# Last layer as one block: the last head group takes half of the sequences first, and the experts start on that half

## The reference, cut to what matters

```
h = rmsnorm(x, ln1_w);  q, k, v = h @ wq, h @ wk, h @ wv          # 16 heads of 128
attn = softmax(where(causal, q @ k.T / sqrt(128), -1e9))
x = x + (attn @ v) @ wo                                            # within each of the 4 sequences
h = rmsnorm(x, ln2_w);  probs = softmax(h @ gate_w.T)              # 16 experts
cw = top 6 of probs, divided by their sum
hh = silu(h @ eg_w.T) * (h @ eu_w.T);  routed = sum_e cw[e] * hh @ ed_w.T
out = x + routed + silu(h @ sg_w.T) * (h @ su_w.T) @ sd_w.T
```

## Time and profile before

| What | us |
|---|---|
| median of three runs | 934.74 |
| the profiled execution | 932.43 |
| its span | 930.7 |
| PE busy | 776.9 (83%) |
| DVE busy | 572.8 (62%) |
| ACT busy | 413.7 (44%) |
| POOL busy | 238.0 (26%) |

### The profile page before, as it was taken

How to read it: one execution, slowest core, us unless ns; L and a number is a source line. 1 busy time by engine, 2 the same in 40 slices (tenths; PEclk the granted TensorE clock), 3 DMA queues, 4 the chain that set the end, 5 groups by cost and what they waited for, 6 DMA issues and landing times. The chain is left out here.

```text
span 930.7 us, 11234 instructions
## 1 busy us (share of the span) xinstructions
PE 776.9 (83%) x3633; PEld 581.3 (62%) x3633; DVE 572.8 (62%) x1269; ACT 413.7 (44%) x856; POOL 238.0 (26%) x245
## 2 busy tenths in 40 slices
PE   1986685887864465999999999999989999999995
PEld 0433454444542155878888787887777888888883
DVE  6997999979989874556555565555635323233333
ACT  6894111244414655545464354543533334343331
POOL 5310101500042412102111021120021555555452
PEclk9998997889977776999999999999977999999998
DMA  4000005723120003011010110000022241333411
GB/s 144 3 0 1 0 0 197 288 69 137 46 73 0 1 1 130 6 46 46 1 46 1 46 46 1 1 1 1 1 69 66 74 114 57 92 78 80 95 38 45
DMA packets 37374, 49.85 MB, mean 54 GB/s; under 512 B 18670, under 2 KB 30038, under 8 KB 35654
## 3 DMA queue, kind: packets, MB, share of 16 engines
q1 hardware_dynamic: 36262, 46.90, 16.5%
q0 software_dynamic: 768, 2.10, 0.7%
q10 hardware_dynamic: 288, 0.14, 0.1%
HBM read 43.00 MB, written 6.13 MB: 53 GB/s over the span
## 5 line engine op out<-in xcount | busy, mean ns | idle before, releaser
L2273 DVE TENSOR_TENSOR B_l<-bank,TW_l 128x512 f32<-128x512 f32 (+1 forms) x50 | 34.6, 692 | 141.0 <-PE bank L2218 141.0
L1891 ACT ACTIVATE EX<-EX,nm 128x128 f32<-128x128 f32 (+1 forms) x128 | 57.2, 448 | 108.5 <-DVE nm L1940 108.0
L1841 POOL TENSOR_TENSOR WL<-RAW,WH 128x512 fp32r<-128x512 f32 x32 | 41.1, 1289 | 228.9 <-ACT WH L1865 228.9
L2308 POOL TENSOR_TENSOR HL_l<-H_l,HH_l 128x512 fp32r<-128x512 f32 (+1 forms) x50 | 64.1, 1283 | 115.2 <-ACT HH_l L2287 115.2
L2218 PE MATMUL bank<-XH,WH_l 128*128 128x512 f32 (+1 forms) x200 | 80.0, 400 | 0.0
L2218 PE MATMUL bank<-XH,WL_l 128*128 128x512 f32 (+1 forms) x200 | 79.7, 399 | 0.0
L2218 PE MATMUL bank<-XL,WH_l 128*128 128x512 f32 (+1 forms) x200 | 79.7, 399 | 0.0
L2295 ACT ACTIVATE S_l<-bank 128x512 f32<-128x512 f32 (+1 forms) x50 | 30.1, 601 | 84.2 <-PE bank L2218 84.2
L1954 DVE TENSOR_TENSOR AL<-bank,AH 128x256 fp32r<-128x256 f32 x64 | 27.1, 424 | 62.1 <-ACT AH L1906 62.1
L155 POOL TENSOR_TENSOR WV<-EUK,V 128x512 f32<-128x512 f32 x16 | 23.7, 1488 | 148.8 <-DVE GAIN L244 114.1
L1995 PE MATMUL bank<-XH,WH 128*128 128x512 f32 x128 | 59.7, 466 | 1.3 <-DVE XL L1695 1.3
(11 more groups left out here) (306 smaller groups left out, 2076.4 us busy)
## 6 DMA issues: line engine op xcount, KB each, us to landing
RAW<-l_attn SPq DMA_DIRECT2D x8, 1024.0 KB, 4.9
WE<-l_experts SPq DMA_DIRECT2D x1, 6144.0 KB, 23.0
RAW_l<-l_experts SPq DMA_DIRECT2D x9, 512.0 KB, 3.8
TW_l<-routed SPq DMA_DIRECT2D x16, 256.0 KB, 5.1
RAW<-l_w SPq DMA_DIRECT2D x3, 1024.0 KB
TW_l<-routed SPq DMA_DIRECT2D x14, 192.0 KB, 3.2
RAW_l<-l_experts SPq DMA_DIRECT2D x9, 256.0 KB, 4.6
sorted_x<-ZERO SPq DMA_DIRECT2D x1, 1920.0 KB, 8.1
```

The costliest lines, as they stand in the source:

```text
L1841: pool.tensor_tensor(WL[:, slot, c], RAW[:, slot, c], WH[:, slot, c].bitcast(F32), ALU.subtract).then_inc(w_low, 1)
L1891: act.activation(EX[:, s, a:b], EX[:, s, a:b], ACT.Exp, bias=nm[:, s, i:i + 1], scale=scale, accum_out=rs[:, s, i:i + 1]).then_inc(expd, 1)
L2273: v.tensor_tensor(self.B[0:rows, q % 2], self.k.banks[2 * (q % 2) + 1][0:rows], self.TW[0:rows, w % self.TWS, n * W:(n + 1) * W], ALU.mult ...
L2308: pool.tensor_tensor(self.HL[0:rows, q % 4], self.H[0:rows, q % 2], self.HH[0:rows, q % 4].bitcast(F32), ALU.subtract).then_inc(self.h_low, 1)
```

## The change

The three blocks become one, `layer3`, so that no engine waits for all others between attention, experts and store. Tiles XH, XL, HN, RAW, WH and WL serve both parts; HH and HL lie where Q and K lay.

The last group has its own list. Its units 0 to 3 are both heads of sequences 0 and 1, units 4 to 7 those of sequences 2 and 3; W0 and W1 are the full output of the first half of tokens. Q (squares), M (sums and means), R (roots and reciprocals) and X (spread, normalise, split) are the second normalisation of that half. ACT splits the first expert's weights in the same group.

```
+LAST_PLAN = """S0 C4 S1 N0 C5 C6 N1 T0 C7 T1 S2 A0 C8 S3 N2 A1 C9 N3 T2 C10 T3 A2 C11 A3
+    S4 W0 S5 W1 N4 Q0 S6 N5 T4 M0 S7 N6 T5 A4 N7 T6 A5 R0 T7 A6 X0 A7 W2 W3""".split()
+LAST_MADE = [0, 1, 2, 3, 4, 5, 8, 10, 6, 7, 9, 11]
+def unit(g, n):
+    return ((n // 2) % 2, 2 * (n // 4) + n % 2) if is_last(g) else (n // 4, n % 4)
+def out_chunk(g, n):
+    return (n % 2, n // 2) if is_last(g) else (n // 2, n % 2)
```

```
+STEPS3[1], STEPS3[2] = STEPS3[2], STEPS3[1]
+ROUTE3, OWN3 = 2, (10, 12, 14, 16)
 # PE, after the last group
+            pe.wait_ge(added, 4 * GROUPS)
+            pe.wait_ge(normb.xl, 2)
+            def ahead(q):
+                if q == ROUTE3:
+                    pe.wait_ge(normb.xl, 4)
+                if q == ROUTE3 + 2:
+                    pe.wait_ge(rt, 10 + 2 * NT)
...
+                    for t in range(NT):
+                        mm = pe.transpose(banks[t // 4][0:EXPERTS3, (t % 4) * P:(t % 4 + 1) * P], CW[:, t], k.IDF[:])
...
+                    pe.wait_ge(rows, 2)
+            def behind(q):
+                if q == 0:
+                    normb.add_up(pe, 1)
+                if q == 1:
+                    normb.spread_out(pe, 1)
...                                                     # router logits into banks[6]
+                if q == 2:
+                    pe.wait_ge(normb.xn, 4)
+                    pe.wait_ge(rt, 2)
 # ACT, after the last group
+            act.wait_ge(added, 4 * GROUPS)
+            normb.squares(act, 1)
+            normb.roots(act, 1)
+            normb.high(act, 1)
+            act.wait_ge(scores, 8 * GROUPS)
+            def ahead(q):
+                if q == ROUTE3:
+                    act.wait_ge(rt, 2)
+                    act.activation(PR[:], LG[:], ACT.Exp).then_inc(ex_, 1)
+                if q == ROUTE3 + 2:
+                    for n in range(2):
+                        act.wait_ge(cw_turned, n + 1)
+                        act.activation(ROWW[:, n * W:(n + 1) * W], banks[n][0:EXPERTS3], ACT.Copy).then_inc(rows, 1)
 # DVE
+            for q in range(len(STEPS3)):
+                if q == ROUTE3:
+                    ex.product(v, q - 1)
+                    routed()
+                ex.weigh(v, q)
+                if q >= 1 and q != ROUTE3:
+                    ex.product(v, q - 1)
+                if q in OWN3:
+                    own(OWN3.index(q))                   # X = X + XC, one chunk
+            ex.product(v, len(STEPS3) - 1)
+            v.wait_ge(owned, NCH)
+            for n, j in enumerate(ORDER):
+                v.wait_ge(ex.down, len(STEPS3) - 1 + n // 2)
+                v.tensor_tensor(chunk(k.X[:], j), chunk(k.X[:], j), banks[4 + j][:], ALU.add).then_inc(summed, 1)
```

More of the change, by code:

```diff
@@ L1646, in __init__ @@
+class Norm:
+    def __init__(self, name, sem, k, tiles, col, sum_banks, spread_banks):
+        self.k, self.t, self.col, self.sum_banks, self.spread_banks = k, tiles, col, sum_banks, spread_banks
         self.sq, self.sums, self.mean, self.root, self.rec, self.spread, self.xn, self.xh, self.xl = [
             sem(f"{n}_{name}") for n in "sq sums mean root rec spread xn xh xl".split()]
-    def squares(self, act, k):
-        for j in ORDER:
-            act.activation(chunk(self.SQ[:], j), chunk(k.XC[:], j), ACT.Square).then_inc(self.sq, 1)
@@ L1655, in scalar @@
[L1655 to L1661, removed]
-            act.wait_ge(self.xn, i + 1)
[L1664 to L1674, removed]
-            j = ORDER[i]
[L1677 to L1690, removed]
@@ L1692, in low, with squares @@
-    def low(self, v, n):
[L1693 to L1714, removed]
+    def squares(self, act, n):
+        for j in ORDER[2 * n:2 * n + 2]:
+            act.activation(chunk(self.t.SQ[:], j), chunk(self.k.XC[:], j), ACT.Square).then_inc(self.sq, 1)
@@ new lines, in add_up, with means @@
+    def add_up(self, pe, n):
+        pe.wait_ge(self.sq, 2 * n + 2)
+        for t in range(4):
+            at = (4 * n + t) * P
+            for h in range(KD):
+                mm = pe.matmul(self.sum_banks[n][:, t:t + 1], self.t.SQ[:, h, at:at + P], self.k.ONES[:, 0:1],
+                               start=(h == 0), stop=(h == KD - 1))
+        mm.then_inc(self.sums, 1)
+    def means(self, v, n):
+        t = slice(4 * n, 4 * n + 4)
+        v.wait_ge(self.sums, n + 1)
+        v.tensor_scalar(self.t.ms[:, t], self.sum_banks[n][:, 0:4], 1.0 / D, EPS3, ALU.mult, ALU.add).then_inc(self.mean, 1)
@@ new lines, in roots, with factors, spread_out @@
+    def roots(self, act, n):
+        t = slice(4 * n, 4 * n + 4)
+        act.wait_ge(self.mean, n + 1)
+        act.activation(self.t.rt[:, t], self.t.ms[:, t], ACT.Sqrt).then_inc(self.root, 1)
+    def factors(self, v, n):
+        t = slice(4 * n, 4 * n + 4)
+        v.wait_ge(self.root, n + 1)
+        v.reciprocal(self.t.rstd[:, t], self.t.rt[:, t]).then_inc(self.rec, 1)
+    def spread_out(self, pe, n):
+        pe.wait_ge(self.rec, n + 1)
+        for t in range(4):
+            mm = pe.matmul(self.spread_banks[n][:, t * P:(t + 1) * P],
+                           self.t.rstd[:, 4 * n + t:4 * n + t + 1].to_broadcast([P, P]), self.k.IDF[:], start=True,
+                           stop=True)
+        mm.then_inc(self.spread, 1)
@@ new lines, in normalise, with high @@
+    def normalise(self, v, n):
+        v.wait_ge(self.spread, n + 1)
+        for j in ORDER[2 * n:2 * n + 2]:
+            v.scalar_tensor_tensor(chunk(self.t.HN[:], j), chunk(self.k.XC[:], j),
+                                   self.t.LN[:, self.col, j // 2:j // 2 + 1], self.spread_banks[n][:], ALU.mult,
+                                   ALU.mult).then_inc(self.xn, 1)
+    def high(self, act, n):
+        for i in (2 * n, 2 * n + 1):
+            act.wait_ge(self.xn, i + 1)
+            j = ORDER[i]
+            act.activation(chunk(self.t.XH[:], j), chunk(self.t.HN[:], j), ACT.Copy).then_inc(self.xh, 1)
@@ L1717, in each_group @@
+    def low(self, v, n):
+        for i in (2 * n, 2 * n + 1):
+            v.wait_ge(self.xh, i + 1)
+            j = ORDER[i]
+            v.tensor_tensor(chunk(self.t.XL[:], j), chunk(self.t.HN[:], j), chunk(self.t.XH[:], j).bitcast(F32),
+                            ALU.subtract).then_inc(self.xl, 1)
 def each_group(eng, body):
@@ L2290, in scalar @@
             p = q - FIRST3[i]
+            ahead(q)
             act.wait_ge(self.gate_up, q + 1)
@@ L2344, in layer3_experts @@
         routed_d = nc.dram_tensor("routed4", (EXPERTS3 + 1, T), F32).ap()
[L2345 to L2351 removed]
+        norm = Norm("l3a", sem, k, tiles, 0, (banks[0], banks[3]), (banks[1], banks[2]))
@@ new lines, in layer3 @@
+        normb = Norm("l3b", sem, k, tiles, 1, (banks[0], banks[4]), (banks[1], banks[5]))
+        raw_in = [sem("raw_in0_3"), sem("raw_in1_3")]
+        (ln_in, mask, w_high, w_low, proj, evac0, evac1, scores, rowmax, negmax, expd, recd, normed, turned,
+         pt, av, ah, al, wo, added) = [sem(n + "_3") for n in """ln_in mask w_high w_low proj evac0 evac1 scores
+            rowmax negmax expd recd normed turned pt av ah al wo added""".split()]
+        r_in, logits, rt, ex_, cw_turned, rows, sent, owned, summed, stored = [
+            sem(n + "_4") for n in ("r_in", "logits", "route", "exps", "turned", "rows", "sent", "owned", "summed", "stored")]
@@ L2353, in layer3_experts, with evacuate @@
+        def evacuate(eng, g, n, do):
+            c = made(g, n)
+            eng.wait_ge(proj, 12 * g + n + 1)
+            if later(g):
+                if c < 4:
+                    eng.wait_ge(scores, 8 * (g - 1) + 4)
+                elif c < 8:
+                    eng.wait_ge(av, 8 * g)
+                else:
+                    eng.wait_ge(scores, 8 * g)
+            do(target(c), banks[n % 2][:]).then_inc(evac[n % 2], 1)
         block = ctx.enter_context(nc.Block())
@@ L2374, in _, with split_high @@
             ex.gpsimd(pool)
+        def split_high(act, g, count, slot, m):
+            act.wait_ge(raw_in[slot], 16 * count)
+            if not isinstance(g, int) or g >= 2:
+                act.wait_ge(wo, 4 * (g - 1))
+            c = slice(m * GCOL, (m + 1) * GCOL)
+            act.activation(WH[:, slot, c], RAW[:, slot, c], ACT.Copy).then_inc(w_high, 1)
         @block.scalar
         def _(act):
-            norm.squares(act, k)
-            for part in range(3):
-                ex.split_high(act, 0, part)
@@ L2381, in _ @@
-            norm.scalar(act, k)
-            act.wait_ge(rt, 2)
-            act.activation(PR[:], LG[:], ACT.Exp).then_inc(ex_, 1)
-            for n in range(2):
-                act.wait_ge(turned, n + 1)
-                act.activation(ROWW[:, n * W:(n + 1) * W], banks[5 + n][0:EXPERTS3], ACT.Copy).then_inc(rows, 1)
-            ex.scalar(act)
+            for n in range(2):
+                norm.squares(act, n)
+            for m in range(4):
+                split_high(act, 0, 1, 0, m)
+            for n in range(2):
+                norm.roots(act, n)
@@ new lines, in _, with evacuated, body @@
```

(69 more changed lines are left out.)

679 lines of the change are left out of this document (309 added, 370 removed).

## The result

The changed kernel takes 929.84 us (median, 928.65 to 930.30), the kernel before beside it 934.90: a ratio of 0.9942, 95% interval 0.9929 to 0.9956, so 5.1 us or 0.6% faster. The profiled execution took 930.3, its span 928.6; it counts among the four. Medians here are over all executions, and the ratios leave out those in a slower state of the chip (two of "store only", one of the kernel before).

The account below looks back on a forecast made before the run. PE sets the end wherever its queue is full, so gains lie in transition and tail: -5.3 (transition) - 4.35 (store) + 2.5 (clock) = -7.15, giving 927.6 us against the 934.74 median; range 921.5 to 932.5, own range 925 to 930.

Parts of the forecast that it names:

- rival B: Transition gives nothing, waits in the last group and DRAM trip undersized by 2 to 3 us each; 930 to 932; chance 0.16.
- step 0 at 41: Sign of being right: first expert step starts some 41 us after the last group's first score matmul, before 55.6.
- step 6 at 77.5: Sign of being right: first plain steady expert step starts 77.5 us after the last group's first score matmul, before 82.8.
- a last group longer than 42 us: Sign of being wrong: the last group of heads, forecast to end at t = 40.3, takes over 42 us.
- The store: End of kernel: two adds beside down 49, two follow; 3.8 us after the last matmul in place of 8.2, 4.35 won.
- The transition: Last group to steady expert steps, without a block end and half the tokens first: step 6 at 77.5 against 82.8, 5.3 won.
- ahead of W2: PE, done at t = 34.75, waits 2.7 us for the last head's subtraction, behind normalisation work on DVE's queue.
- ahead of step 4: PE waits 2.15 us, from t = 63.8, for ACT's copies to ROWW.
- ahead of down 3: PE waits 3.15 us: weights return from DRAM at t = 72.7, then weigh 4, product 3, copy and POOL's 1.28.
- The clock: Half clock on PE after three waits over 2 us in dense work; taken as 2.5 us lost, bounds 0 and 15.
- Rival A: The clock never falls or the waits are shorter: -9.65 and a bit, 922 to 925 us; chance 0.17.
- C: Rival: PE stays at half clock for 10 us after each of three waits, 15 lost, +5.4, 940 us; chance 0.07.

Follow-up runs that it names:

- store only: Kernel before with only the store's part: XC added into X beside expert steps 10 to 16, four closing adds instead of eight; 932.58 us, ratio 0.9968.
- old tail: Changed kernel with the end of before: no adds of XC into X beside the steps, eight adds in a row after the last down product; 934.36 us, ratio 1.0001.
- product 3 first: Changed kernel with one swap on DVE, product 3 ahead of weigh 4; 923.96 us, ratio 0.9885.
- filled wait: Changed kernel with 10 matmuls of 512 columns, into a bank nothing reads any more, in PE's wait ahead of W2; 930.39 us, ratio 0.9959.

## Why the prediction was right in size and wrong in its parts

Forecast 927.6, measured 929.84: inside 921.5 to 932.5, and faster, to which I gave 0.82. But it lies just under rival B's 930 to 932, whose account ("only the store is won") is what the traces show. That the time still fell inside the range is luck: the store alone gives 930.4, which lies in it too. Of the signs I named, step 0 at 41 and step 6 at 77.5 did not come (44.7 and 82.7), and one of the signs of being wrong did: a last group longer than 42 us.

- **The store**: 4.35 forecast, 4.2 in the trace (8.2 to 4.0). Right, and the runs bear it out: with the old tail the gain is nil; the adds alone, on the kernel before, give 2.5.
- **The transition**: 5.3 forecast before the clock, measured 0.1 with it. This is the step that failed. Its waits were the right ones, in the right places and with the right causes (ahead of W2 2.7 said, 2.64 measured; ahead of step 4 2.15 and 1.68; ahead of down 3 3.15 and 3.76; trip from the copies to the landing 6.8 and 7.1). What was mis-sized is the list between them, and step 6 came 5.2 later than I said:
  - Up to step 0, 3.5. W2 came at t = 39.7, not 37.5: the second half of the group started at 20.3, not 18.9, and lost another 0.9 up to W2. The half clock over W2 and W3 added 1.3. I take it that the hand-overs from PE to DVE or ACT and back, which I had rounded to the modelled ends of the instructions, add up over the dozens in the group; that was not tested by itself.
  - From step 0 to the landing of the weights, 0.8 (32.3 for 31.5). DVE took 5.2 us from Exp to the weights, where I had taken 4.24 from before. Two of its instructions are the difference: the making of CW took 0.87 and its scaling 0.71, both 0.29 before. In the changed kernel POOL's subtractions run beside them; before, POOL did nothing yet.
  - From the landing to step 6, 0.9. POOL's subtraction ahead of down 3 took 1.80 in place of 1.28, with DVE's product 5 beside it, and down 3 took 1.7 in place of 1.4, the last of it at half clock.
- **The clock**: 2.5 forecast. In the profiled execution three stretches at half clock lengthened PE's work: 1.3 over W2 and W3, 1.6 over step 2, 1.5 behind down 3, 4.4 in all. But the 1.6 did not reach step 6: DVE is in the routing until 717.4, step 3, late by the 1.6, ends at 717.5, and DVE's weigh 3 behind weigh 2 needs it only then. PE waits 1.68 for what follows from there. And the tail ran at full clock (0.39 against 0.61 in the earlier trace rows) behind a wait of 2.13, before 2.14, which gives back 1.4 (from its first to its last matmul 2.6 us, before 4.0); I had said that its low clock stays. One of the three falls I had in the wrong place: step 2, behind no wait longer than 0.64 (the logits ahead of it are 32 matmuls of 16 columns), not behind step 4's.
- **Sum by parts**: of the falls, 1.3 over W2 and W3 and 0.2 in down 3 stand on the way to step 6. Without them the transition would be worth 1.6 of the forecast 5.3; the missing 3.7 are the list, 2.2 of it in the group and the rest behind step 0. This is an estimate from one profile: in those of "filled wait" and "old tail", step 0 comes 1.2 earlier and step 6 still at 83.1.
- **Rival A**: not seen. **C** needed 10 us at half clock behind each wait; each of the changed kernel's falls lasted some 3, and the longest in the other kernels 6.8.
- Of the two rules of the Trainium skill that I weighed: the drain of 1.38 us behind a table load ("ScalarE: Activation LUTs", section "What ACT_TABLE_LOAD costs") again doesn't show. Four loads here, each with the next instruction at its end, as in the lines below. The trip through DRAM took 7.1 us, of which 1.9 lie between the issue of the write and that of the reads: the rows were the better guide here too.

```profile
706.70 1.28 ACT L2033 ACT_TABLE_LOAD   x1
708.00 1.09 ACT L2033 ACTIVATE S_l<-bank 128x512 f32<-128x512 f32 x2
```

The two instructions of DVE that took longer, and POOL beside them; that one lengthens the other is read from the times alone, but in the profiles of "product 3 first", "filled wait" and "old tail", where POOL's subtraction starts later than it, the first of the two takes 0.29:

```profile
715.22 0.87 DVE L2377 SCALAR_TENSOR_TENSOR CW<-REP,PR 128x128 f32<-128x128 f32 x1
716.67 0.71 DVE L2383 TENSOR_TENSOR CW<-CW,tot 128x128 f32<-128x128 f32 x1
```

```profile
714.64 1.29 POOL L2046 TENSOR_TENSOR HL_l<-H_l,HH_l 128x512 fp32r<-128x512 f32 x1 [2.06 <-ACT HH_l L2024]
715.89 1.34 POOL L1941 TENSOR_TENSOR WL<-RAW,WH 128x512 fp32r<-128x512 f32 x1
```

What the forecast missed in kind: I listed the wait ahead of down 3 as a price and did not see that it was one line's order. It was worth 5.9 us (5.3 by the ratios), as much as the whole change.

Open: why the clock falls behind one wait of 2.64 and not behind the same wait in two other executions, and behind the tail's 2.14 but not its 2.13. The filled wait did not settle it, and each kernel's places come from one profile.

## What to carry to other kernels

When blocks are merged, list for each engine what now stands behind the first wait for a slow thing (here weights that go to DRAM and back), and move ahead of it all that doesn't need it: that was worth 5 to 6 us here, as much as the whole change, store included. Work brought forward is not yet won, since new waits behind it can spend it: compare the place of the first steady step, not of the first step. And look at the tail by itself: here it was the whole gain, and four adds that could be made earlier were about half of it.

## What I had not expected

- With the last group's old order, one block put step 6 at 86.5, the three blocks at 82.8: leaving out the blocks' ends did not help as such. Bare waits of 3.0 and 3.8 us and half clock took their place.
- The clock was low over step 2 in seven of the eight profiles of kernels with one block, around 3.6 to 4.0 us of 16-column matmuls and a wait of 0.3 to 0.64. In "product 3 first", "filled wait" and "old tail" it fell while these matmuls still ran, ahead of that wait: from t = 55.3 to 55.6 it is 0.50 in all three, and step 2 starts at 56.1 to 56.2. It did not fall behind the wait of 1.3 to 2.2 ahead of step 4 in any of the six that have it.
- The earlier layers, with the same instructions, differ by up to 5.4 us between profiles (the last group starts at 648.3 to 653.7), as much as most edits here are worth. Places are comparable when counted from a common matmul, absolute times are not.
